# Cross-attention of a post-norm decoder layer: values of 1024 columns in place of values fused with the output projection

## The reference

```
q = (x @ Wq);  k = (context @ Wk);  v = (context @ Wv)       # heads of 64
attn = softmax(q k^T * 64**-0.5)
out  = concat over heads (attn v)                            # 64 x 1024
return out @ Wo + bo                                         # 64 x 128
```

## Time and profile before

| | us |
|---|---|
| median of 3 runs (lowest, highest) | 885.01 (880.82, 885.24) |
| the profiled execution's own time | 882.52 |
| its span, first to last instruction | 880.8 |
| TensorE busy | 783.5 (89%) |
| VectorE, ScalarE, GpSimd busy | 632.1, 593.7, 452.0 |
| mean granted TensorE clock | 0.981 |

### The profile page before, as it was taken

The page is one execution under the profiler, slowest core; times in us unless marked ns, Lnnn a source line. Parts: engine busy times, 40 slices in busy tenths (PEclk is TensorE's granted clock), DMA queues, the critical chain, the costliest instruction groups (busy, mean ns, idle before and its releaser), DMA issues.

```text
span 880.8 us, 26463 instructions
## 1 busy us (share of the span) xinstructions
PE 783.5 (89%) x9205; PEld 654.3 (74%) x9237; DVE 632.1 (72%) x1898; ACT 593.7 (67%) x1444; POOL 452.0 (51%) x440
## 2 busy tenths in 40 slices
PE   4799999999999988999999999999997877687776
PEld 3577777778787767888888878788886767677752
DVE  3878778878787757778787878788888555445425
ACT  2677878888787856777676767777766454455535
POOL 5477676776767632223535353535342545554443
PEclk9899999999999999999999999999999999889998
DMA  8499999000000000000000000000002455556636
GB/s 282 82 157 161 158 156 121 2 0 0 0 0 0 2 1 6 7 7 7 27 10 28 10 28 9 24 13 25 12 22 73 136 166 175 159 177 184 204 104 231
DMA packets 69505, 65.30 MB, mean 74 GB/s; under 512 B 5689, under 2 KB 54972, under 8 KB 69280
## 3 DMA queue, kind: packets, MB, share of 16 engines
q1 hardware_dynamic: 62592, 51.42, 28.5%
q0 software_dynamic: 4736, 10.12, 3.3%
q10 hardware_dynamic: 2080, 2.49, 0.9%
HBM read 35.88 MB, written 28.58 MB: 73 GB/s over the span
## 4 chain that ended last, share of the span: by engine, by line
PE 51%; issue 20%; POOL 12%; ACT 6%; DVE 6%; DMA 3%; another core or an unknown queue 1%; SPq 1%; POOLq 0%; ACTq 0%; DVEq 0%
PE bank L1791 7%; PE bank L1687 7%; PE bank L1487 6%; PE bank L1489 5%; PE bank L1488 5%; POOL rq L530 5%; PE bank L1662 3%; PE bank L1675 3%; POOL PR L535 3%; PE bank L1801 3%; PE bank L1563 2%; PE bank L1571 2%; ACT VBD L391 2%; PE bank L1781 1%; POOL rs L544 1%
## 5 line engine op out<-in xcount | busy, mean ns | idle before, releaser
L391 ACT COPY VBD<-bank 64x512 f32<-64x512 f32 x192 | 111.2, 579 | 28.5 <-PE bank L1489 25.8
L567 POOL TENSOR_TENSOR PR<-PR,rL 128x1024 f32<-128x1024 f32 x32 | 60.9, 1902 | 115.7 <-DVE rL L1114 115.6
L530 POOL TENSOR_TENSOR rq<-ssq,mhalf 128x17 f32<-128x17 f32 x32 | 99.2, 3100 | 15.7 <-DVE ssq L963 15.1
L627 POOL DMA_INDIRECT zbuf<-PT,KT x71 | 69.8, 983 | 72.3 <-ACT PT L889 50.2
L535 POOL TENSOR_TENSOR PR<-PR,rL 128x1024 f32<-128x1024 f32 x32 | 60.9, 1904 | 82.4 <-DVE rL L994 82.4
L1417 DVE SCALAR_TENSOR_TENSOR stage<-bank,b_now,early 128x128 f32<-128x128 f32 x142 | 43.1, 345 | 61.9 <-ACT early L881 46.2
L1791 PE MATMUL bank<-xT,w_now 128*128 128x128 f32 x568 | 82.7, 292 | 0.4 <-DMA w_now<-in_wl 0.3
L619 POOL DMA_INDIRECT xbuf<-xg,slot x64 | 64.9, 1014 | 34.3 <-DVE xg L1283 21.8
L881 ACT ACTIVATE early<-bank,b_now 128x128 f32<-128x128 f32 x142 | 44.4, 367 | 56.3 <-PE bank L1791 38.4
L1791 PEld LDWEIGHTS bank<-xT,w_now 128*128 128x128 f32 x568 | 73.8, 203 | 1.6 <-issue 1.3
L797 ACT ACTIVATE PT<-bank 128x512 f32<-128x512 f32 x64 | 38.3, 600 | 43.3 <-PE bank L1675 41.5
(11 more groups left out here) (243 smaller groups left out, 2338.8 us busy)
## 6 DMA issues: line engine op xcount, KB each, us to landing
w_now<-in_wl SPq DMA_DIRECT2D x71, 256.0 KB
xbuf<-blank SPq DMA_DIRECT2D x1, 17160.0 KB, 120.5
KT<-xbuf SPq DMA_DIRECT2D x71, 65.0 KB
VBD<-zbuf SPq DMA_DIRECT2D x4, 512.0 KB, 5.1
out<-X SPq DMA_DIRECT2D x8, 256.0 KB, 2.3
cT<-in_ctxT ACTq DMA_DIRECT2D x16, 96.0 KB, 2.0
zbuf<-PT,KT POOLq DMA_INDIRECT x71
wl_sb<-in_wl POOLq DMA_DIRECT2D x1, 1024.0 KB, 9.3
```

The costliest lines, as they stand in the source:

```text
L391: u = copy(VBD[h * SEQ:(h + 1) * SEQ, p, s, lo:lo + blocks, :], bank[CHUNK_BANK[c]][s * SEQ:(s + 1) * SEQ, :].rearrange("k (a d) -> k a d" ...
L530: nc.gpsimd.tensor_tensor(rq[:, :], ssq[:, :], mhalf[:, 0:HEADS + 1], ALU.pow).then_inc(a["pow"], 1)
L567: nc.gpsimd.tensor_tensor(v, v, rL[:, p, :].unsqueeze(2).broadcast_to([P, HEADS, SEQ]), ALU.mult)\
L627: nc.gpsimd.indirect_dma_start(out=zbuf, out_offset=at, in_=yb[:, t % YB, :], in_offset=None, bounds_check=K2 * TOK - 1, oob_is_err=False) ...
```

## The change

The weights are no longer fused. The value of a context token has 1024 columns, two chunks of 512 per tile (`b_v`). The weighted sums are products of their own (`b_o`): per tile 32 quarter tiles, 64 keys x 64 value columns with 64 query columns, half of the heads into bank 4 and half into bank 5. They are copied to OT, one bank by ScalarE, the other by VectorE (`b_oT`). The output projection (`b_y`) is 32 quarter tiles of 64 x 64 with 128 columns that accumulate in banks 1 and 5, and VectorE adds bank 5 and X, then bank 1 (`b_add_y`). GpSimd adds the bias to X beforehand (`add_bo`). Wo is loaded twice, once with its halves swapped; Wv goes through the same split as Wq and Wk, two more slices. In the loop, `b_add_y` stands one iteration earlier, `b_tail_b` in every iteration behind the first max, two key chunks behind `b_y`, and one value chunk behind it. The score block waits for `r` (the first add) in place of PT, since bank 5 is read there.

```diff
-        xwvT_sb = early[:, 0:NBLK * CD].rearrange("p (a c) -> p a c", a=NBLK)
-        xwo_sb = early[:, W:2 * W].rearrange("p (a d) -> p a d", a=NBLK)
-        sg = early[:, W:W + W // 2].rearrange("p (b h) -> p b h", b=2)
-        vo_hi, vo_lo = sb("vo_hi", [CD, NVO, HW], F32R), sb("vo_lo", [CD, NVO, HW], F32R)
+        xwv_hi, xwv_lo = sb("xwv_hi", [CD, W], F32R), sb("xwv_lo", [CD, W], F32R)
+        xwo_sb = sb("xwo_sb", [P, NBLK, D])
+        xwo_swap = sb("xwo_swap", [P, NBLK, D])
+        sg = sb("sg", [P, 2, HID])
...
 
-        def b_u(copy, eng, t, p, c):
-
-
-            eng.wait_ge(b["u"], NVO * t + c + 1)
-            if later(t, 2):
-                eng.wait_ge(b["y"], t - 1)
-            blocks, h = HVO, c // 2
-            lo = (c % 2) * blocks
-            for s in range(PB):
-                u = copy(VBD[h * SEQ:(h + 1) * SEQ, p, s, lo:lo + blocks, :],
-                         bank[CHUNK_BANK[c]][s * SEQ:(s + 1) * SEQ, :].rearrange("k (a d) -> k a d", a=blocks))
-            u.then_inc(b[f"u{c}"], 1)
+        def b_v(copy, eng, t, c):
+
+
+            p, h = c // 2, c % 2
+            eng.wait_ge(b["v"], 2 * t + c + 1)
+            if later(t + p, 2):
+                eng.wait_ge(b["o"], 2 * (t + p - 1))
+            for n in range(PB):
+                v = copy(VBD[h * SEQ:(h + 1) * SEQ, p, n, :, 0:DH],
+                         bank[CHUNK_BANK[c]][n * SEQ:(n + 1) * SEQ, :].rearrange("k (a d) -> k a d", a=NBLK))
+            v.then_inc(b[f"v{c}"], 1)
+
+        def b_oT(copy, eng, t, h):
+
+            eng.wait_ge(b["o"], 2 * t + h + 1)
+            if later(t, 1):
+                eng.wait_ge(b["y"], 2 * t)
+            copy(OT[:, :, h * SEQ:(h + 1) * SEQ], bank[4 + h][:, :].rearrange("d (a q) -> d a q", a=NBLK))\
+                .then_inc(b[f"oT{h}"], 1)
...
+            def add_bo(t):
+                if t == 0:
+                    pool.wait_ge(w_cross, 16)
+                pool.wait_ge(b["xs"], t + 1)
+                nc.gpsimd.tensor_tensor(X[:, t, :], X[:, t, :], bo_sb[:, :], ALU.add).then_inc(b["xb"], 1)
...
                     b_q(i, 3)
+                stage_of(lambda t, q: b_oT(nc.scalar.copy, act, t, 0), i, p, 2)
+                if pair:
                     b_k(nc.scalar.copy, act, i, 0)
-                    b_k(nc.scalar.copy, act, i, 2)
-                if p == 1 and has(i):
-                    b_u(nc.scalar.copy, act, i - 1, 0, 2)
+                if fresh:
+                    b_v(nc.scalar.copy, act, i - 1, 2)
                 if (g := due(i, T_at)) is not None:
                     route_T(g)
-                if p == 1 and has(i):
-                    for c in (0, 1, 2, 3):
-                        b_u(nc.scalar.copy, act, i, 1, c)
+                if pair:
+                    b_k(nc.scalar.copy, act, i, 2)
+                if fresh:
+                    b_v(nc.scalar.copy, act, i - 1, 3)
...
-            def b_add_y(t, p, bk=1):
-                dve.wait_ge(b["y"], t + 1)
-                V.tensor_tensor(r1[:, :], bank[bk][:, 0:D], X[:, bass.ds(t, 1), :].rearrange("q a d -> q (a d)"),
-                                ALU.add).then_inc(b["r"], 1)
+            def b_add_y(t, p):
+                dve.wait_ge(b["y"], 2 * (t + 1))
+                dve.wait_ge(b["xb"], t + 1)
+                V.tensor_tensor(r1[:, :], bank[5][:, 0:D], X[:, t, :], ALU.add).then_inc(b["r"], 1)
+                dve.wait_ge(b["r"], t + 1)
+                V.tensor_tensor(r2[:, :], bank[1][:, 0:D], r1[:, :], ALU.add).then_inc(b["rb"], 1)
 
             def b_stats(t, p):
-                dve.wait_ge(b["r"], t + 1)
-                V.tensor_tensor(r2[:, :], r1[:, :], bo_sb[:, :], ALU.add).then_inc(b["rb"], 1)
...
                 stage_of(lambda t, q: b_max(t, q, 1), i, p, 1)
-                if p == 1 and has(i):
-                    stage_of(b_add_y, i, p, 3)
-                    b_u(V.tensor_copy, dve, i - 1, 0, 1)
-                    stage_of(b_sum, i, p, 1)
-                    b_u(V.tensor_copy, dve, i - 1, 0, 3)
-                    stage_of(b_stats, i, p, 3)
-                else:
-                    stage_of(b_add_y, i, p, 3)
-                    stage_of(b_stats, i, p, 3)
-                    stage_of(b_sum, i, p, 1)
-                    stage_of(b_tail_b, i, p, 3)
+                if fresh:
+                    b_v(V.tensor_copy, dve, i - 1, 1)
+                stage_of(b_sum, i, p, 1)
+                stage_of(lambda t, q: b_oT(V.tensor_copy, dve, t, 1), i, p, 2)
                 if pair:
                     b_k(V.tensor_copy, dve, i, 1)
+                stage_of(b_add_y, i, p, 2)
+                stage_of(b_stats, i, p, 2)
+                if pair:
...
 
-            def b_uv(t, p, c):
-                if p:
-                    pe.wait_ge(b[f"u{c}"], t)
-                else:
-                    pe.wait_ge(b[f"kT{c}"], t // 2 + 1)
-                    if c == 3:
-                        pe.wait_ge(b["xlo"], T if isinstance(t, int) and t + 2 >= T else t + 4)
-                three(bank[CHUNK_BANK[c]][:, :], cT_hi[:, p, :], cT_lo[:, p, :], vo_hi[:, c, :], vo_lo[:, c, :])\
-                    .then_inc(b["u"], 1)
+            def b_v(t, c):
+                p, h = c // 2, c % 2
+                pe.wait_ge(b[f"kT{c}"], t // 2 + 1)
+                if c == 3:
+                    pe.wait_ge(b["xlo"], min(t + 4, T))
+                cols = slice(h * HW, (h + 1) * HW)
+                three(bank[CHUNK_BANK[c]][:, :], cT_hi[:, p, :], cT_lo[:, p, :], xwv_hi[:, cols], xwv_lo[:, cols])\
+                    .then_inc(b["v"], 1)
...
 
-            def b_y(t, p, bk=1):
+            def b_o(t, p):
                 pe.wait_ge(b["pT"], 2 * (t + 1))
-                for c in range(NVO):
-                    pe.wait_ge(b[f"u{c}"], t + 1)
-                if later(t, 1):
-                    pe.wait_ge(b["r"], t)
+                for h in range(2):
+                    pe.wait_ge(b[f"v{2 * p + h}"], t // 2 + 1)
                 for k in range(NBLK):
-                    for s in range(PB):
-                        m = M(bank[bk][s * SEQ:(s + 1) * SEQ, 0:D], PT[:, k * P + s * SEQ:k * P + (s + 1) * SEQ],
-                              VBD[:, p, s, k, :], start=(k == 0), stop=(k == NBLK - 1))
-                m.then_inc(b["y"], 1)
+                    for h in range(2):
+                        r = slice(h * DH, (h + 1) * DH)
+                        for s in range(PB):
+                            half = s if h == 0 else 1 - s
+                            m = M(bank[4 + h][half * DH:(half + 1) * DH, k * SEQ:(k + 1) * SEQ], VBD[r, p, s, k, 0:DH],
+                                  PT[r, k * P + s * SEQ:k * P + (s + 1) * SEQ], start=True, stop=True)
+                        if k == NBLK - 1:
+                            m.then_inc(b["o"], 1)
+
+            def b_y(t, p):
+                for h in range(2):
+                    pe.wait_ge(b[f"oT{h}"], t + 1)
+                if t == 0:
+                    pe.wait_ge(w_xo, 48)
+                if later(t, 1):
+                    pe.wait_ge(b["rb"], t)
+                lo, hi = slice(0, DH), slice(DH, P)
+                even, odd = slice(0, SEQ), slice(SEQ, 2 * SEQ)
+                for k in range(NBLK):
+                    g = dict(start=(k == 0), stop=(k == NBLK - 1))
+                    M(bank[1][0:SEQ, 0:D], OT[lo, k, even], xwo_sb[lo, k, :], **g)
+                    m0 = M(bank[1][SEQ:P, 0:D], OT[lo, k, odd], xwo_swap[lo, k, :], **g)
+                    M(bank[5][0:SEQ, 0:D], OT[hi, k, odd], xwo_sb[hi, k, :], **g)
+                    m1 = M(bank[5][SEQ:P, 0:D], OT[hi, k, even], xwo_swap[hi, k, :], **g)
+                m0.then_inc(b["y"], 1)
+                m1.then_inc(b["y"], 1)
 
...
+                if pair:
                     b_q(i, 0)
                     b_q(i, 1)
                 if p == 1 and has(i + 1):
                     bx_T(i + 1, 0)
                     bx_T(i + 2, 1)
-                if p == 1 and has(i):
-                    b_uv(i - 1, 0, 0)
-                    b_uv(i - 1, 0, 1)
+                if fresh:
+                    b_v(i - 1, 0)
                 stage_of(lambda t, q: b_pT(t, q, 1), i, p, 2)
-                if p == 0 and has(i):
-                    for c in (2, 3):
-                        b_q(i, c)
-                    for c in range(4):
-                        b_k(i, c)
-                if p == 1 and has(i):
-                    for c in (2, 3):
-                        b_uv(i - 1, 0, c)
+                if pair:
+                    b_q(i, 2)
+                    b_q(i, 3)
+                if fresh:
+                    b_v(i - 1, 1)
+                stage_of(b_o, i, p, 2)
+                if pair:
+                    b_k(i, 0)
+                    b_k(i, 1)
+                if fresh:
+                    b_v(i - 1, 2)
                 stage_of(b_y, i, p, 2)
                 if (g := due(i, T_at)) is not None:
...
-                if p == 1 and has(i):
-                    for c in range(NVO):
```

(45 more changed lines are left out.)

52 lines of the change are left out of this document (17 added, 35 removed).

## The result

The changed kernel takes **955.44 us** (median of 4 runs, 952.54 to 956.59); the kernel before, beside it on the same chip, 884.87 (4 runs). The ratio is 1.080 [1.076, 1.084]. The forecast was 918, range 893 to 934: slower was right, the size was half of what came. The profiled run took 954.65 us with a span of 952.9, against 882.5 and 880.8.

A forecast was written before the change was run, and what follows sets the result against it. TensorE's queue was taken as the bound. 15 pairs at +2.20 gave +33 us, routing -1, contention +2, the remaining terms together +1: +35 on the profiled 882.5, 917.5, stated as 918, range 893 to 934.

The forecast's parts named there:

- TensorE's work: Cross-attention, per pair of tiles: fused-value products -2.9 us, weighted sums +2.2, y at 1.90 (2.18 and 3.80 kept open).
- The 0.7 less per pair: Cross-attention: TensorE's own work per pair of tiles becomes 0.7 us smaller, alone making the kernel a little faster.
- The three waits: TensorE idles in odd iterations 1.3 us ahead of b_o and 1.2 ahead of y; odd score blocks wait about 1.
- The iterations: Plain cross-attention iterations: even 11.95 us against 10.55, odd 10.85 against 10.05; pair 22.80 against 20.60, +2.2.
- +2 for the contention of the context split: VectorE's context split meets GpSimd's bias additions in the six groups that also send: +0.4 us each, +2.
- -1 for routing: Cross-attention routing groups: 3.25 us each in the changed kernel against 3.4 before, so -1 us.
- The clock: Sign of being wrong: TensorE's clock leaves 1.00 in the cross-attention stretch as the waits grow; no size given.
- The last part: The span after the scores of tile 31: forecast +1 us.
- the first part: The span up to the scores of tile 2: forecast +1 us.
- TensorE was not the bound: Rival 1, cross-attention: TensorE stays the bound, pair near 19.0 us, -24 us, 859; chance 0.07.
- neither wait was absent: Rival 2: the wait ahead of y or ahead of the scores is absent, +1.1 us per pair, 885 to 898; chance 0.08.
- y overlapped as forecast: Against rival 3: projection in quarter tiles overlaps no better than now, +57 us, 975; chance 0.05.

The follow-up runs named there:

- plain sends: Every indirect GpSimd send made a plain write of the same rows to a fixed place: changed kernel 907.77 us, kernel before 857.56 us.
- all three versions with the keys ahead of y and indirect sends: Changed kernel with the last two key products ahead of y: 958.39 us; plus OT copies on ScalarE: 949.20; plus both those copies and early sends: 968.04.

## Why the prediction failed

- **TensorE's work**: its parts were right. y took 1.91 (taken 1.90), the weighted sums 1.09 (1.09). The 0.7 less per pair is not seen in busy time, which is 303.3 with plain sends against 302.8; busy time also counts the modelled end of the last matmul ahead of each wait, and there are more waits now. The prediction set 17 ns against the 60 cycles (an estimate of 25 ns) that the Trainium skill (TensorEngine Tiling (Array Packing), Instruction Overhead) gives each matmul. But 17 ns is the time of a record, and two records are one matmul of the program: 34 ns, four tiles side by side. So these rows neither show nor refute that figure.
- **The three waits**: right in place and nearly in size: ahead of y 1.34 (1.2), ahead of the scores 1.09 (1.0), ahead of b_o 0.94 (1.3). Undone singly, the first shortened the plain odd iterations by 1.0, the second the plain even ones by 0.8.
- **The iterations**: too short by 0.42 and 0.35. In the even one I ended the second half of the keys at y's end + 1.42 and gave the copy's handoff 0.12. The last key product starts 374.03, its copy at 374.35 and the score block at 375.41, 0.37 after the copy's end. In the odd one the value copies took 1.43, not 1.30, and the sum started 6.08 after the score block, not 5.84. Pair +2.97 rather than +2.20: with 14.5 pairs, **11 us**.
- **Where it failed: the sum's +2 for the contention of the context split and -1 for routing**, all that I gave to the groups with sends beyond the pairs. I priced the additions, and never asked what GpSimd's indirect sends do beside a y that now ends among them. They cost 24.7 us in this stretch where they cost 8.7: **16 us**. The contention with the additions is part of that: I priced it at 0.4 in six groups, it is 0.84 in five, and none with plain sends. Of what is left with plain sends (48.7 - 14.5 x 2.97 = 5.6) I had +1, so **5** more: routing costs a group of four tiles 3.0 us in the changed kernel and 2.3 in the one before, where I had 3.25 against 3.4.
- **The clock**: I named its leaving 1.00 as a sign of being wrong and gave it no price. The 20.5 us at half clock from tile 2 on cost about 5: the group at 0.91 took 2.4 more than the one at 1.00, two others, with 3.4 us at half clock each, 0.7 to 0.8. Most of this is in the 16, as with plain sends they are 3.4.
- **The last part** was +6.0, not +1; 2.8 of it remains with plain sends. Not followed further.
- Terms of 11, 16 and 5 make the 32 us missed in the stretch (+64.7 against +33); the rest of the miss is the 5 behind tile 31. The sum itself, 917.5 for the profiled run, is 920 for the median with its 2.5, not 918. For the 0.9 us of fewer early loads there is no row; the first part as a whole came to +1.4.
- **The rivals** stayed out: TensorE was not the bound, neither wait was absent, and y overlapped as forecast.

The range was too narrow because it held only bounds on durations of plain iterations. From the ninth iteration on, every one carries sends, routing or both.

## What to carry to other kernels

Work out a plain iteration, then the busiest one as well, with each engine's side jobs (here GpSimd's DMA issues) laid beside the new critical handoffs; the second was worth more than the first. Price idle time of TensorE at the clock too: where it already waits, taking work away can cost time, and unread work can win some back. And look for what else a fix moved: with the copies on ScalarE the late adds fell from 17 to 6, so its gain is not all from the wait that it was to remove. Test a fix in the full kernel before counting on what its plain iterations show: all three versions with the keys ahead of y and indirect sends gave back more than the keys had saved.

## What the runs showed of the hardware

- Beside an indirect send of GpSimd (1.0 us each) TensorE's 64x64 matmuls stop for 0.2 to 0.4 us, 0.25 to 0.5 and again 0.9 to 1.3 us after its start, and what waits for y goes on 0.7 to 0.9 us late, 1.3 to 1.5 us after that start. A plain write of the same rows (0.58 us) does neither. The Trainium skill (SBUF — State Buffer, SBUF: two separate sides) says that TensorE never waits for another at the engines' ports, so by it the port is not the cause; these runs don't tell what is.
- Half of TensorE's weighted sums left out, 0.55 us per tile: 9 us slower; 0.5 us of unread products in their place: 7 us faster again. Half of the projection left out, which did not lengthen TensorE's waits: 40 us faster, half-clock time unchanged.
- 3.4 us at half clock lengthened a plain iteration of the half sums by 1.3 us (12.49 against 11.20), and a group of four tiles of the changed kernel by 0.7 to 0.8.
